# A weighted neighbour sum in one pass: the order of one-hots, sums and dense products, and where the edge weight is applied

## What is computed

```python
src, dst = (edge_index[0], edge_index[1])
msg = edge_weight[:, None] * x[src]
agg = jax.ops.segment_sum(msg, dst, num_segments=N)
out = (1.0 + EPS) * x + agg
h = jax.nn.relu(out @ W1 + b1)
return h @ W2 + b2
```

## Time and profile before

| what | value |
|---|---|
| median of 3 runs | 6412.9 us (6406.72 to 6414.36) |
| the profiled execution, its own time | 6421.66 us |
| its span | 6420.0 us |
| the second layer's pass, in the span | from about 1984 to 2979 us |

### The profile page before, as it was taken

One profiled execution on the slowest core, in us unless ns is written; L12 is line 12 of the kernel. 1 busy time (PEld: TensorE's weight loads), 2 busy tenths in 40 slices (PEclk: granted clock), 3 DMA queues, 4 the chain that ended last, 5 costly groups with the idle time before them and its releaser, 6 DMA issues. The chain is left out here.

```text
span 6420.0 us, 85568 instructions
## 1 busy us (share of the span) xinstructions
PE 4893.6 (76%) x27978; PEld 3217.1 (50%) x28217; DVE 3024.8 (47%) x7067; ACT 1631.5 (25%) x2948; POOL 2466.8 (38%) x2476
## 2 busy tenths in 40 slices
PE   1677665997995666666798799989978967777775
PEld 0444333444443334443654376657656556676762
DVE  5678776882005433344546633252242354444445
ACT  0467772001004544443101100010010022222222
POOL 2000000000004743440355177557717727777770
PEclk6799887998996667778799899999999989899987
DMA  2166898997982222221565688798868755555541
GB/s 61 45 83 123 134 143 173 202 204 167 202 180 70 51 54 68 70 60 45 154 198 170 213 263 257 215 278 254 249 211 254 241 147 143 142 143 144 142 116 41
DMA packets 1528180, 980.88 MB, mean 153 GB/s; under 512 B 694462, under 2 KB 1454185, under 8 KB 1527787
## 3 DMA queue, kind: packets, MB, share of 16 engines
q1 hardware_dynamic: 1199263, 626.08, 39.7%
q0 software_dynamic: 90032, 209.15, 11.9%
q10 hardware_dynamic: 238556, 141.40, 7.6%
HBM read 658.95 MB, written 163.25 MB: 128 GB/s over the span
## 5 line engine op out<-in xcount | busy, mean ns | idle before, releaser
L1221 PE MATMUL ps<-adj_d,xs_d 128*128 128x512 bf16 (+1 forms) x7699 | 1702.0, 378 | 163.8 <-DVE xs_d L1180 150.7
L1221 PEld LDWEIGHTS ps<-adj_d,xs_d 128*128 128x128 bf16 x7938 | 781.9, 100 | 1022.7 <-DVE xs_d L1180 154.5
L1135 POOL DMA_INDIRECT rows_d<-xh_tab,src_idx x688 | 698.7, 1016 | 443.7 <-POOLq L168 222.2
L2349 POOL DMA_INDIRECT rows_m<-p_tab,idx_m x784 | 751.9, 959 | 281.9 <-issue 238.4
L780 PE MATMUL ps<-hot,lo 128*128 128x500 bf16 (+4 forms) x2052 | 539.1, 387 | 302.8 <-DVE hot L711 159.3
L1135 POOL DMA_INDIRECT rows_d<-x_tab,src_idx x488 | 487.9, 1000 | 643.1 <-POOLq L168 383.4
L822 ACT CAST slab<-ps 128x1000 f32 (+4 forms) x530 | 558.1, 1053 | 373.0 <-PE ps L798 167.5
L1541 POOL DMA_INDIRECT rows_g<-x_tab,src_idx x492 | 472.7, 961 | 413.1 <-PE ps L1676 287.9
L1700 PE MATMUL ps<-hot_g,lo_w_g 128*128 128x490 bf16 (+1 forms) x876 | 290.5, 473 | 300.2 <-DVE hot_g L1638 159.1
L2476 PE MATMUL ps<-win_m,turned_hot_m 128*128 128x128 f32 x1568 | 338.4, 300 | 191.1 <-DVE pre_m L2416 186.7
L711 DVE TENSOR_SCALAR hot<-iota_key,key_col 128x1225 bf16<-128x1225 int16 (+4 forms) x782 | 414.4, 561 | 110.1 <-PE ps L798 69.8
(11 more groups left out here) (361 smaller groups left out, 6776.3 us busy)
## 6 DMA issues: line engine op xcount, KB each, us to landing
adj_d<-adjacency SPq DMA_DIRECT2D x196, 896.0 KB
attr_m<-in_edge_attr SPq DMA_DIRECT2D x195, 256.0 KB
xp_g<-x_tab SPq DMA_DIRECT2D x56, 448.0 KB
k_rows_d<-k_tab ACTq DMA_DIRECT2D x56, 448.0 KB, 4.7
loc_m<-loc_rows SPq DMA_DIRECT2D x196, 128.0 KB
adjacency<-slab SPq DMA_DIRECT2D x4, 4900.0 KB
q_s<-q_tab SPq DMA_DIRECT2D x42, 448.0 KB
rden_s<-rden_tab SPq DMA_DIRECT2D x42, 448.0 KB
```

Of the source, the lines that this page charges most:

```text
L1135: nc.gpsimd.indirect_dma_start(rows[:, q % GR * K + k, :], None, table, bass.IndirectOffsetOnAxis(ap=src_idx[:, j:j + 1], axis=0)).then_in ...
L1221: last = nc.tensor.matmul(ps[:, m % 2, 0:w], xs[:, g * GW + k, e, :], adj[:, slot, k, 0:w], start=(g == 0 and k == 0 and e == 0), stop=(g ...
L2349: nc.gpsimd.indirect_dma_start(rows[:, q, k, :], None, p_tab, bass.IndirectOffsetOnAxis(ap=idx[:, q, k:k + 1], axis=0)).then_inc(rows_in[2 ...
```

## The change

It is in `layer1_pass`, with changes to constants and counts in the preparation of the edges:

- the strip units get five classes instead of two, the first 28 tiles with width 5 and tiles 140 to 195 with width 7; tile numbers per unit and the chunks stay;
- one-hots of the strips have 8 slots, and `pick` runs five tiles ahead (`EARLY`);
- `match` compares and multiplies by the edge weight in one instruction, and ScalarE's `scale` is gone; TensorE waits for the gathered rows themselves;
- sums of groups have three PSUM banks (`BANK`), and `add(q - 1)` stands where `add(q)` stood;
- groups are spread by columns of TensorE's work, the sweeps included, so that three to five of them stand between the seven parts of each sweep, on TensorE and in VectorE's order;
- x is loaded into three buffers, and the slab is cleared in seven pieces, each after the part of the product that read it.

```diff
-WT, WPAIRS, WNARROW = 292, 70, 49
+WCLASSES = (WClass(0, 28, 2, 5), WClass(28, 98, 2, 7), WClass(98, 140, 2, 10), WClass(140, 196, 1, 7), WClass(196, 292, 1, 10))
+WT, WPAIRS = 292, 70
...
+                        for c in WCLASSES:
+                            at = WUNIT_OF[c.begin]
+                            to = WROW if c.end == WT else WUNIT_OF[c.end]
+                            nc.vector.memset(w_room[:, 0, at:to], float(c.width)).then_inc(strip_done, 1)
+                            nc.vector.memset(w_room[:, 1, at:to], float(WC - c.width)).then_inc(strip_done, 1)
...
-            GR, OH, AHEAD, BANKS, HOTS, XS = 10, 6, 4, 2, 3, 2
+            GR, OH, AHEAD, LAG, HOTS, EARLY, XS = 10, 6, 4, 1, 8, 5, 3
+            BANK = (0, 1, 7)
...
+                    widths = [WIN * TERMS * WUNITS[WUNIT_OF[t]].width for t in range(WT)]
+                    step = GW * 320
+                    total = sum(widths) + len(WFIRSTS) * G * step
...
+                        after_tile.append(groups * work // total)
+                        if t in sweep_at:
+                            for g in range(G):
+                                work += step
+                                after_part.append(groups * work // total)
...
-                            if c:
-                                act.wait_ge(x_used, c * G)
-                            nc.scalar.copy(slab[:, :, :], zero[:, 0:1].unsqueeze(2).to_broadcast([P, WIN, WC])).then_inc(blank, 1)
-
-                        def scale(q):
-                            act.wait_ge(rows_in[q % GR], 16 * K * (q // GR + 1))
-                            for k in range(K):
-                                j = (first_group + q) * K + k
-                                last = nc.scalar.activation(rows[:, q % GR, k, :], rows[:, q % GR, k, :], ACT.Copy, scale=ew_col[:, j:j + 1])
-                            last.then_inc(scaled, 1)
+                            for g in range(first, end):
+                                if c:
+                                    act.wait_ge(x_used, (c - 1) * G + g + 1)
+                                nc.scalar.copy(slab[:, g * GW:(g + 1) * GW, :], zero[:, 0:1].unsqueeze(2).to_broadcast([P, GW, WC])).then_inc(blank, 1)
...
+                            if t in blank_at:
+                                blanken(blank_at[t], 0, 4)
+                            if t - 1 in blank_at:
+                                blanken(blank_at[t - 1], 4, G)
...
-                                last = nc.vector.tensor_scalar(onehot[:, q % OH, k, :], iota16[:, :], loc_col[:, j:j + 1], None, ALU.is_equal)
+                                last = nc.vector.tensor_scalar(onehot[:, q % OH, k, :], iota16[:, :], loc_col[:, j:j + 1], ew_col[:, j:j + 1],
+                                                               ALU.is_equal, ALU.mult)
...
-                            dve.wait_ge(blank, chunk_of[u] + 1)
+                            dve.wait_ge(blank, (chunk_of[u] + 1) * G)
...
+                        for t in range(EARLY):
+                            pick(t)
                         for q in range(AHEAD):
                             match(q)
                         for t in range(WT):
-                            pick(t)
+                            pick(t + EARLY)
...
+                            for q in range(before_tile[t], before_tile[t + 1]):
                                 match(q + AHEAD)
-                                add(q)
+                                if q >= LAG:
+                                    add(q - LAG)
...
-                            if q >= BANKS:
-                                pe.wait_ge(added, after_group[q - BANKS])
-                            pe.wait_ge(scaled, q + 1)
+                            if q >= len(BANK):
+                                pe.wait_ge(added, after_group[q - len(BANK)])
+                            pe.wait_ge(rows_in[q % GR], 16 * K * (q // GR + 1))
...
+                                for q in range(q, after_part[n]):
+                                    sum_group(q)
+                                q = after_part[n]
```

More of the change, by code:

```diff
@@ L60 @@
 AC = N + max(COLUMNS) + 6
-WT, WPAIRS, WNARROW = 292, 70, 49
+WClass = namedtuple("WClass", "begin end tiles width")
+WCLASSES = (WClass(0, 28, 2, 5), WClass(28, 98, 2, 7), WClass(98, 140, 2, 10), WClass(140, 196, 1, 7), WClass(196, 292, 1, 10))
+WT, WPAIRS = 292, 70
 WUnit = namedtuple("WUnit", "tile tiles width")
-WUNITS = [WUnit(2 * k, 2, 7 if k < WNARROW else 10) for k in range(WPAIRS)]
-WUNITS += [WUnit(t, 1, 10) for t in range(2 * WPAIRS, WT)]
+WUNITS = [WUnit(t, c.tiles, c.width) for c in WCLASSES for t in range(c.begin, c.end, c.tiles)]
 WUNIT_OF = [k for k, u in enumerate(WUNITS) for n in range(u.tiles)]
@@ L554, in _ @@
                         done(8)
[L555 to L558, removed]
+                        dve.wait_ge(strip_done, 27)
+                        for c in WCLASSES:
+                            nc.vector.scalar_tensor_tensor(out=w_key[:, c.begin:c.end], in0=hi_f[:, c.begin:c.end], scalar=float(c.width),
+                                                           in1=w_key[:, c.begin:c.end], op0=ALU.mult, op1=ALU.add).then_inc(strip_done, 1)
                         for c in CLASSES:
@@ L1498, in layer1_pass @@
                     rows_in, x_in = s[0:GR], s[GR:GR + XS]
-                    (tabs_in, listed, cleared, terms, matched, scaled, group_done, added, hot_made, lo_made, lo_weighted, stripped, entered,
+                    (tabs_in, listed, cleared, terms, matched, group_done, added, hot_made, lo_made, lo_weighted, stripped, entered,
                      blank, x_used) = s[GR + XS:]
-                    due = [[] for t in range(WT)]
-                    for q in range(groups):
-                        due[q * WT // groups].append(q)
@@ new lines, in layer1_pass @@
+                    step = GW * 320
+                    total = sum(widths) + len(WFIRSTS) * G * step
+                    after_tile, after_part, work = [], [], 0
+                    for t in range(WT):
+                        work += widths[t]
+                        after_tile.append(groups * work // total)
[3 more added lines that the diff above has]
+                                after_part.append(groups * work // total)
@@ L1512, in layer1_pass @@
                         if t in place_at:
                             after_place.append(len(after_group) + len(after_place) + 1)
+                    for q in range(groups - LAG, groups):
+                        after_group.append(len(after_group) + len(after_place) + 1)
                     def sums_of(q):
-                        return ps[:, q % BANKS, 0:P]
+                        return ps[:, BANK[q % len(BANK)], 0:P]
                     def strip(u):
@@ L1703, in _ @@
                                 last.then_inc(stripped, 1)
-                            for q in due[t]:
+                            for q in range(before_tile[t], after_tile[t]):
                                 sum_group(q)
                             if t in sweep_at:
-                                sweep(sweep_at[t])
-                        sweep(len(WFIRSTS) - 1)
+                                sweep(sweep_at[t], after_tile[t])
         def layer1_nodes():
```

42 lines of the change are left out of this document (21 added, 21 removed).

## The result

The changed kernel takes 6069.6 us (median of 4 runs, 6065.73 to 6072.12); the kernel before, run beside it, takes 6413.6 (4 runs, 6406.72 to 6416.81). The ratio is 0.946, with a 95% interval of 0.945 to 0.948: 344 us are gone. Forecast were 6049 us, with a range of 6036 to 6130. The profiled execution took 6065.73 us with a span of 6064.1.

A forecast was written before the change was run, and what follows sets the result against it. It took a ring of waits between engines to bound the pass, with GpSimd's gathers next: 6421.66 - 365 for the pass + 1 for preparation = 6058 us profiled, 6049 as a median, range 6036 to 6130.

The forecast's parts named there:

- The ring: Waits in the pass from VectorE's add through one-hots, ScalarE's weighing and TensorE's products to the next add: period 5.86 us.
- the gathers as the next bound: Without the closed chain of waits, GpSimd's gathers set the pace at 5.0 us a group; chance 0.72.
- adding a group late, with one-hots five tiles ahead, cuts the ring: In the pass, VectorE at group q waits only for q-1; with gathers then setting the pace, 365 us gained.
- the sweeps at zero: Sweeps with groups inside were to cost nothing, and up to 30 us without the slots of rows.
- what is late behind them: After seven sweeps, a clearing piece, weighing and entry delay TensorE 2 to 3 us each: 20 us if not covered.
- The rows: Term for the pass: 491 remaining gathers at 1.257 us end at 2610, the pass at 2614, gaining 365 us.
- The rival of ports for the small one-hots: Each of VectorE's 492 group one-hots holds up a gather by its length: 109 us, 6158 as a median; chance 0.05.
- the large one: Every VectorE instruction of the pass holds up gathers for its length: 393 us added, 6442 us; chance 0.03.
- the rule for two-port modes: Skill's rule against the change: VectorE in such a mode and GpSimd exclude each other; 3 us expected in all.
- 600 us by the old share of clock levels: TensorE's work in the pass with 44% of time at the full clock level, taken as hidden under the gathers.
- The rival in which gaps keep its clock low: TensorE becomes the bound of the pass with 644 to 768 us of work: median 6097 to 6221; chance 0.17.
- its wait at the add would be small: Sign in the pass: VectorE's wait at a group's add is small or for the previous group.

The follow-up runs named there:

- a_three_gathers: Changed kernel with three gathers instead of four per group, the fourth tile's product rereading the third's rows: 5930.0 us, pass 509.1 us, first chip.
- a_scale_rows: Changed kernel with edge weights applied by ScalarE to the gathered rows again and a plain one-hot: 6783.2 us, pass 763.5 us, third chip.
- a_again_2: The changed kernel itself, run again unaltered on the third chip: 6786.6 us, ratio 0.961 to the kernel before, pass 763.4 us.
- b_ring_cut: Kernel before with only early one-hots in eight slots, third bank and late add: 7007.6 us, ratio 0.986, second chip; repeated on the third, 6976.1 us, 0.988.
- a_lag0: Changed kernel with the add of a group back at its old place, one-hots still five tiles ahead: 6837.8 us, pass 775.6 us, second chip.
- a_early1_lag0: Changed kernel with adds not late and one-hots one tile ahead in three slots: 6867.6 us, pass 806.3 us, second chip.

## Why the prediction was right, and where its 21 us went

**The ring, and the gathers as the next bound: right.** POOL's wait for TensorE fell from 288 us to 1.8, the pass from 993 to 630.6, where I had said about 630. The gain in the pass is 363 us, forecast 365. a_three_gathers shows the bound. This holds for the first chip. On the other two the changed kernel gains 251 and 269 us in all, its pass takes 772 and 763, and TensorE is seven to nine groups behind the gathers at each sweep but the last; the forecast knew nothing of such chips, and it was luck that the first runs fell on one without the pauses.

**But what cut the ring was only partly what I named.** I priced the gain at the step "adding a group late, with one-hots five tiles ahead, cuts the ring". I had the sweeps at zero, up to 30 us without the slots, and what is late behind them at 20 us "if not covered". With early one-hots the late add is worth nothing; taking both out costs 34 us of the pass; and the two put in alone give about a third of the gain. All of this was measured on the second and third chip. The rest hangs on the new spread, pieces, buffers and widths, which I had priced at nothing or not at all. The sum came out because all parts were there and the bound under them was right. It could not have told what each is worth, and that the parts priced at nothing were in the change too is luck.

**The rows.** 1.259 us a gather, forecast 1.257. One of the rows that I gave for it says something else: 1992.79 to 1995.45 for two gathers is 1.33 us each, since the first few take 1.07 us and not 0.94; the 80 in 100 us carry the 1.25. Beside a VectorE that is 64% busy the gathers without the first took (475.9 - 7.14)/491 = 0.955 us; I had 0.014 over 0.940 and got 0.015. The rival of ports for the small one-hots wanted 109 us more, the large one 393, and both fall. One long instruction does hold up a gather: 7.14 us with the memset beside it, 1.22 without. The Trainium skill ("SBUF — State Buffer", section "SBUF: two separate sides") gives the shared port pair to a VectorE instruction in a two-port mode or with two SBUF inputs. Of one with at most one SBUF input, outside these modes, it says that it does not contend with GpSimd; it names copy, cast and `tensor_scalar` as those that can enter a two-port mode, and not the memset. The memset of 5.39 us did hold the gather, and the measurement decides. The 492 one-hots of 0.36 are `tensor_scalar` instructions, and beside them the gathers took 0.955 us against the shortest 0.940, so the trace hardly shows the rule there. My prediction called the memset an agreement with the rule for two-port modes; it is one only if a memset is in such a mode, which no run here shows. The rows of the last group were in use 3.0 us after their gather's instruction ended (2619.02 - 2615.98), where I had bounded it by 1.9: 1 us.

**TensorE.** Busy 453 of 630.6 us at 0.87. I had 600 us by the old share of clock levels, and took it as hidden. The rival in which gaps keep its clock low falls: with fewer gaps the clock rose.

**VectorE.** 0.360 us for the one-hot with the weight, between my 0.296 and 0.403; I had taken the lower end, and 492 x 0.064 = 31 us lie under the gathers. That its wait at the add would be small was wrong: 121 us, mostly inside sweeps, up to 6.0 each. It costs nothing.

**ScalarE.** 325 us, forecast 337; the 56 clearings take 57.1 us between my bounds of 48.6 and 67.6. Scaling was worth nothing (a_scale_rows).

**Sweeps.** 20 to 28 us forecast; the eight take 17.3 to 23.2, three of them under 20, and the last 19.3 (2597.71 to 2617.04, where its last part ends). Groups inside the sweeps are worth 16 us, all at the last one.

**The 21 us.** The pass was 1.9 us longer than forecast. It began 5.1 us later (1990.47 against 1985.35), of which the preparation, the part that the change touches, has 0.2; it had been given 1. What follows the pass took 1.7 us more. That is 8 us for the profiled execution. The other 12.7 are the step from it to the median: I subtracted 8.8 us, as the profiled execution before was that far above its median, and the one after was 3.9 below its own. Stages that no edit touches moved by up to 6 us ahead of the pass and by 9 behind it from one kernel to the next on the first chip, so this step had no better answer than a bound of about 10 us on either side, which my own range lacked.

## What to carry to other kernels

When no engine is full, close the chain of waits into a period, then look for the engine that issues at a fixed cost and count its instructions: 492 of them at the 1.259 us between starts are 619 of the pass's 630.6 us, whatever the parts did. Cutting a ring of waits gives this bound only if the order of work also keeps the buffers of that engine from filling, so check where a long stretch without its consumer stands (here a sweep and a clearing), and how much of the work is spent before it. A sum that comes out right over several edits says nothing about each; here two of them, the late add and the scaling, were worth nothing on the chips where they were taken out one at a time.

## What the runs showed of the hardware

**Two chips on which these kernels take longer.** The kernel before takes 11 and 10% longer there than on the first chip (7098.3 and 7055.5 to 6411.7), the changed kernel 13 and 12% (6847.6 and 6786.6 to 6069.6). Up to the start of this pass nothing differs (it begins between 1984.8 and 1990.5 us on all three). From 2011 us on, VectorE and GpSimd pause together. Rows of the timeline of a_again_2:

```profile
2303.21 0.52 DVE L1664 TENSOR_TENSOR slab_g<-slab_g,ps 128x343 f32 x1 [4.81 <-remote]
2303.30 0.94 POOL L1558 DMA_INDIRECT rows_g<-x_tab,src_idx  x1 [1.92 <-remote]
...
2314.95 0.94 POOL L1558 DMA_INDIRECT rows_g<-x_tab,src_idx  x1 [1.88 <-remote]
...
2326.56 0.94 POOL L1558 DMA_INDIRECT rows_g<-x_tab,src_idx  x1 [1.93 <-remote]
```

Here the pause comes every 11.6 or 11.7 us and lasts 1.9; elsewhere in the pass most come 11.6 to 12.0 or 17.3 to 18.0 us after the one before, and most last 1.8 to 2.8, the first 7.1. The releaser is not in the profile of this core. 138 gathers start in 200 us, where the first chip has 160. The traces of the first chip have no such rows. Its cause is open.

It bears on the experiments of the second and third chip. A gather there takes 200/138 = 1.45 us of the span, and still TensorE doesn't keep up. When a sweep of a_again_2 other than the last starts, 7 to 9 groups are gathered that TensorE hasn't used (32 to 25 at the first). TensorE never waits for rows, and the pass ends 38.8 us after the last gather's start. On the first chip the changed kernel has at most one such group, waits 136 us for rows, and ends after 6.0. So on the second and third chip the strips' side is the late one, with POOL's slots nearly full, and what an edit of TensorE's or VectorE's order is worth there may be more than on the first chip. b_ring_cut, a_lag0, a_early1_lag0 and a_scale_rows have been measured only there.

**VectorE's long memset holds a gather that is being issued**, 7.14 us against 1.22, while a copy of the same size on ScalarE does not.
